# Turning a tile's gathered rows with a DMA transposition instead of TensorE, in a GRU scan that feeds a mixture of experts

## What is computed

```python
# x: [16, 256, 512]; h starts from cond_2048 [16, 512]; D = 512
def cell(h, x):                        # GRU, 256 steps, one after the other
    gi = x @ W_ih + b_ih               # [16, 1536]
    gh = h @ W_hh + b_hh
    r, z = sigmoid(i_r + h_r), sigmoid(i_z + h_z)
    n = tanh(i_n + r * h_n)
    return (1.0 - z) * n + z * h
# the 4096 rows h go through a mixture of 8 experts, top 2 of 8, hidden width 352
scores = h @ Wg.T;  w = softmax of the two best scores
for e in range(8):
    y += w[:, e] * ((silu(h @ W1[e].T) * (h @ W2[e].T)) @ W3[e].T)
out = x + y
```

## Time and profile before

| | us |
|---|---|
| median of 3 runs | 1501.19 (1500.92 to 1502.19) |
| span of the profiled execution | 1501.1 |
| TensorE matmuls, busy | 1409.4 (94% of the span) |
| VectorE, busy | 1043.8 (70%) |
| ScalarE, busy | 896.3 (60%) |
| GpSimd, busy | 415.8 (28%) |

### The profile page before, as it was taken

The page is one execution under the profiler, slowest core; times in us unless marked ns, Lnnn a source line. Parts: engine busy times, 40 slices in busy tenths (PEclk is TensorE's granted clock), DMA queues, the critical chain, the costliest instruction groups (busy, mean ns, idle before and its releaser), DMA issues.

```text
span 1501.1 us, 88729 instructions
## 1 busy us (share of the span) xinstructions
PE 1409.4 (94%) x37804; PEld 1227.2 (82%) x37804; DVE 1043.8 (70%) x4116; ACT 896.3 (60%) x2319; POOL 415.8 (28%) x850
## 2 busy tenths in 40 slices
PE   2888878899999999999999999999999999998997
PEld 1888778888888888888888888888888888885664
DVE  7788887777677677777777767776777776764333
ACT  6677675555565556655556555665556655555664
POOL 1011112123322232222332223222333222326443
PEclk9999887899999999999999999999999999999999
DMA  8445413112221222212222122211222212223431
GB/s 290 124 130 140 134 45 90 40 32 40 46 39 39 46 46 40 39 39 46 40 46 40 39 46 46 41 38 40 46 40 46 40 39 47 39 40 79 60 49 16
DMA packets 99011, 88.64 MB, mean 59 GB/s; under 512 B 41407, under 2 KB 74175, under 8 KB 98624
## 3 DMA queue, kind: packets, MB, share of 16 engines
q0 software_dynamic: 17952, 33.64, 12.9%
q1 hardware_dynamic: 80672, 49.32, 11.5%
HBM read 59.12 MB, written 35.72 MB: 63 GB/s over the span
## 4 chain that ended last, share of the span: by engine, by line
PE 83%; DVE 10%; issue 3%; ACT 1%; POOL 1%; DMA 1%; SPq 0%; DVEq 0%; POOLq 0%; ACTq 0%
PE gn_bank L1366 12%; PE gz_ps L1366 12%; PE y_ps L1458 9%; PE b_ps L1388 9%; PE a_ps L1422 8%; PE b_ps L1422 8%; PE gi_ps L1388 8%; PE gr_ps L1357 6%; PE gr_ps L1351 6%; DVE wexp L1037 2%; PE tr_ps L1436 2%; PE tr_ps L1446 2%; PE tr_ps L1478 1%; DVE npre L1067 1%; DVE nmh L1073 1%
## 5 line engine op out<-in xcount | busy, mean ns | idle before, releaser
L1366 PE MATMUL gz_ps<-hlog,whh 128*128 128x32 f16 x8192 | 246.0, 177 | 6.1 <-issue 6.0
L1366 PE MATMUL gn_bank<-hlog,whh 128*128 128x32 f16 x8192 | 245.2, 177 | 2.4 <-issue 2.2
L625 POOL DMA_INDIRECT out_y<-work,mt x57 | 93.9, 1648 | 546.2 <-PE gz_ps L1366 309.6
L1366 PEld LDWEIGHTS gz_ps<-hlog,whh 128*128 128x128 f16 x8192 | 224.1, 96 | 6.9 <-issue 6.7
L1366 PEld LDWEIGHTS gn_bank<-hlog,whh 128*128 128x128 f16 x8192 | 224.2, 96 | 2.7 <-issue 2.7
L1351 PEld LDWEIGHTS gr_ps<-hlog,whh 128*128 128x128 f16 x4096 | 130.6, 96 | 53.9 <-DVE hlog L1080 32.4
L1351 PE MATMUL gr_ps<-hlog,whh 128*128 128x16 f16 x4096 | 141.9, 170 | 31.3 <-DVE hlog L1080 28.3
L1388 PE MATMUL b_ps<-xs,wih 128*128 128x64 f16 x4752 | 162.3, 197 | 3.4 <-issue 2.1
L1458 PE MATMUL y_ps<-wexp,work 128*128 x639 | 159.0, 382 | 1.9 <-ACT work L845 1.9
L1388 PEld LDWEIGHTS b_ps<-xs,wih 128*128 128x128 f16 x4752 | 153.3, 101 | 5.1 <-issue 3.5
L810 ACT ACTIVATE rs<-rpre,sc 128x64 f32<-128x64 f32 x256 | 88.0, 344 | 112.7 <-DVE rpre L1054 112.5
(11 more groups left out here) (217 smaller groups left out, 2550.3 us busy)
## 6 DMA issues: line engine op xcount, KB each, us to landing
wexp<-in_w_units SPq DMA_DIRECT2D x46, 256.0 KB, 3.8
x_raw<-in_x_feat SPq DMA_DIRECT2D x32, 256.0 KB, 3.7
out_y<-in_x_tok SPq DMA_DIRECT2D x16, 512.0 KB
h_tok<-xrow SPq DMA_DIRECT2D x32, 256.0 KB, 2.0
wexp<-in_w_hh SPq DMA_DIRECT2D x4, 768.0 KB, 6.8
wexp<-in_w_inproj SPq DMA_DIRECT2D x4, 768.0 KB, 11.8
wexp<-in_w_units SPq DMA_DIRECT2D x15, 192.0 KB, 4.5
mt<-meta SPq DMA_DIRECT2D x71, 1.0 KB, 1.7
```

The lines of the kernel that those rows point to most:

```text
L625: pool.indirect_dma_start(out=out, out_offset=bass.IndirectOffsetOnAxis(ap=mt[:, j % RING, 0:1].bitcast(I32), axis=0), in_=ysc[y_slot(j)], ...
L1366: mm = pe.matmul(dst[:, j], whh[:, i, k, m * P:(m + 1) * P], h[:, k], start=False, stop=True, skip_group_check=True)
```

## The change

The block X disappears from TensorE and `take_x` from ScalarE. SyncE issues one DMA transposition a tile, `turn_gathered(j)`, from xg to xT, two steps before the tile's block A. It waits until the gather has landed and until block B of the tile that used the same xT buffer has ended. Block A and the gather into the same xg buffer now wait for its semaphore. In the tail SyncE's loop is: turn_gathered(j), then take_up(j+2). The inner activations (T) and the rows of h (R1) are turned on TensorE as before.

```diff
         if g >= 0 and s in (2, ranked):
             work += [("R1" if s == 2 else "R2", g)]
-        if (t + 1 - FIRST) % CYCLE == 0 and t + 1 >= FIRST:
-            work += [("X", (t + 1 - FIRST) // CYCLE)]
...
         if j + 1 < TILES:
-            tail += [("E", j + 1), ("X", j + 1)]
+            tail += [("E", j + 1)]
...
-        x_mm = sem("x_mm")
-        x_taken = sem("x_taken")
+        gathered_turned = [sem(f"gathered_turned_{i}") for i in range(2)]
...
+            def turn_gathered(j):
+
+                sp.wait_ge(x_gathered[j % 4], 16 * (j // 4 + 1))
+                if j:
+                    sp.wait_ge(b_mm, j if j <= MAIN_TILES else j - 1)
+                sp.dma_start_transpose(xT[x_slot(j)], xg[g_slot(j)]).then_inc(gathered_turned[j % 2], 16)
+
...
                         take_up(j)
                         if j == MAIN_TILES:
                             take_up(j + 1)
-
-            for j in range(MAIN_TILES + 2, TILES):
-                if stage(j) == LAST and stage(j - 1) < LAST:
-                    store_rows(LAST)
-                take_up(j)
+                    elif t == base(j) - 2:
+                        turn_gathered(j)
+
+            take_up(MAIN_TILES + 2)
+            for j in range(MAIN_TILES + 1, TILES):
+                turn_gathered(j)
+                if j + 2 < TILES:
+                    if stage(j + 2) == LAST and stage(j + 1) < LAST:
+                        store_rows(LAST)
+                    take_up(j + 2)
...
                 if j - 3 > MAIN_TILES:
-                    pool.wait_ge(x_mm, j - 3 - MAIN_TILES)
+                    pool.wait_ge(gathered_turned[(j - 3) % 2], 16 * ((j - 3) // 2 + 1))
                 elif j > MAIN_TILES:
                     pool.wait_ge(gi_mm, GI_BATCHES)
                 elif j:
-                    pool.wait_ge(tr_mm, TR_NO["X", j - 1] + 1)
+                    pool.wait_ge(gathered_turned[(j - 1) % 2], 16 * ((j - 1) // 2 + 1))
...
-            def take_x(j):
-                if j:
-                    act.wait_ge(b_mm, j if j <= MAIN_TILES else j - 1)
-                dst = xT[x_slot(j)].rearrange("p c t -> p (c t)")
-                if j <= MAIN_TILES:
-                    act.wait_ge(tr_mm, TR_NO["X", j] + 1)
-                    S.copy(dst, tr_ps[:]).then_inc(tr_taken, 1)
-                else:
-                    act.wait_ge(x_mm, j - MAIN_TILES)
-                    S.copy(dst, gn_bank[:].bitcast(F16)).then_inc(x_taken, 1)
...
                 if w == 0:
-                    if j <= MAIN_TILES:
-                        pe.wait_ge(tr_taken, TR_NO["X", j] + 1)
-                    else:
-                        pe.wait_ge(x_taken, j - MAIN_TILES)
+                    pe.wait_ge(gathered_turned[j % 2], 16 * (j // 2 + 1))
...
-            def turn_x(j):
-                pe.wait_ge(x_gathered[j % 4], 16 * (j // 4 + 1))
...
-                for c in range(2 * K):
-                    mm = pe.transpose(dst[:, c * P:(c + 1) * P], xg[g_slot(j)][:, c * P:(c + 1) * P], ident[:])
-                mm.then_inc(tr_mm if j <= MAIN_TILES else x_mm, 1)
```

More of the change, by code:

```diff
@@ L156, in gru_moe_kernel @@
             tail += [("T", j - 1)]
-    TR_NO = {b: n for n, b in enumerate([b for b in main + tail if b[0] in ("T", "R1")
-                                              or b[0] == "X" and b[1] <= MAIN_TILES])}
+    TR_NO = {b: n for n, b in enumerate([b for b in main + tail if b[0] in ("T", "R1")])}
     ROUTED_BEFORE_A, BATCH_BEFORE_B, B_BEFORE_BATCH = {}, {}, {}
@@ L925, in _ @@
                     probabilities(t // GS - 1)
-                if t >= FIRST - 1 and s == CYCLE - 1:
-                    take_x(j + 1)
                 if t % GS == 6 and t // GS + 2 < UNITS_X:
@@ L938, in _ @@
                 gate_sigmoid(j)
-                if j + 1 < TILES:
-                    take_x(j + 1)
                 if j > MAIN_TILES:
@@ L1531, in run @@
                     turn_hidden(n)
-                elif kind == "X":
-                    turn_x(n)
                 elif kind == "D0":
```

## The result

The changed kernel takes 1490.42 us (median of 5, 1489.49 to 1497.22) beside 1501.19 of the kernel before (1499.14 to 1502.82, timed again on the same chip). The ratio is 0.9943 [0.992, 0.9965]: 8.6 us by the ratio and 10.8 by the medians, where 25.5 were forecast. The time lies in the slower part of the stated range and the sign was right, but the gain is only a third to two fifths of what the sum promised.

A forecast was written before the change was run, and what follows sets the result against it. TensorE's queue was taken to bound scan and steady tail. Scan -21.4 and tail -4.1 (head +2.5, steady tail -6.6) sum to -25.5 us from 1501.1: 1475.5 us forecast, range 1470 to 1497 (80%).

The forecast's parts named there:

- Block X, 0.42 us x 51 = 21.4: Scan: each removed block of TensorE transpositions frees 0.42 us, for 51 blocks 21.4 us; bounds 18.4 to 23.5.
- L = 5.0: DMA transposition's time from issue on SyncE to its semaphore, taken as 5.0 us, between estimates 3.4 and 5.7.
- the 1024 pieces: Assumption that a transposition reads 1024 pieces of 256 B, 128 rows by eight blocks of 128 columns.
- Hidden in the scan: Scan: transposition starts some 12 us before block A wants it, so L up to 12 us costs nothing.
- The added DMA traffic ... nothing: Scan: 1024 more packets in 20 us beside a DMA share of 0.21 were costed at nothing.
- The steady tail, 6.6: Behind A(55): 15 tile periods, each 0.44 us shorter without X, gain 6.6 us.
- The head, +2.5: Start of the tail: A(55) starts 2.5 us later because transpositions delay the chain of gathers.
- 2L - 7.5: Tail's head: delay of A(55), transposition paid twice, in GpSimd's queue and between gather and A.
- gives nothing: Last scan step: removing the 52nd block, X(51), gains nothing, since R1 behind it waits for H_LO anyway.
- The drain behind the last tile is the same: End of the kernel: the time behind the last tile was taken as unchanged.
- about 10 us of the 11.7 that two tiles last: Steady tail: mt and gather behind the transposition take about 10 us of 11.7, so hidden without much room.
- SyncE held so long in issuing that mt is late: Listed sign that the forecast is wrong: SyncE's issuing of transpositions makes the row-number load mt late; no size given.

The follow-up runs named there:

- e2: Kernel before with DMA transposition only for tail tiles 52 to 70, TensorE still turning the scan's tiles: ratio 1.0041 to the kernel before.
- e14: Kernel before with the scan's 51 DMA transpositions added and TensorE's block X kept: ratio 1.0019 to the kernel before.
- e9: Changed kernel run again unedited, on another set's chip: ratio 0.9936 to the kernel before.
- e1: Changed kernel with the tail of before: DMA transposition only for scan tiles 0 to 51: ratio 0.9922 to the kernel before.
- e15: Scan-only kernel again (DMA transposition in the scan, TensorE turning the tail), in another set: ratio 0.9909 to the kernel before.
- e3: Changed kernel with mt issued ahead of the transposition in the tail, last h_tok store and transposition 54 before the list wait: ratio 0.9879 to the kernel before.
- e6: Changed kernel with GpSimd's tail loop issuing add_rows(j-2) ahead of gather(j+4): ratio 0.9884 to the kernel before.
- e12: Scan-only kernel with no turning of rows in the scan at all, so output differs: ratio 1.0406 to the kernel before.
- e7: Changed kernel with gather(53) waiting until transposition 52 has ended: ratio 0.9904 to the kernel before.
- e8: Changed kernel with both tail reorderings, mt ahead of the transposition and add ahead of the gather: ratio 0.9886 to the kernel before.
- e10: Changed kernel with gather(53) waiting for transposition 52 and tail adds issued ahead of gathers: ratio 0.9871 to the kernel before.
- e11: Scan-only kernel with each scan transposition replaced by a plain copy of the same 256 KB, rows unturned: ratio 0.9907 to the kernel before.

## Why the forecast missed

- **Block X, 0.42 us x 51 = 21.4:** right. It took 21.2 (before) and 20.9 (e2) of TensorE, and the step behind it moves up by all of that.
- **L = 5.0:** right, 4.7 in the scan and 4.4 over all, and so were the 1024 pieces behind it. Hidden in the scan: right, no wait of block A for it shows there.
- **"The added DMA traffic ... nothing":** wrong. The forecast asked who waits for the transfer, and not whom it delays. By e14 some 3 us, by the other pairs up to 5, of the 21.4 come back in stops of TensorE. That TensorE waits in such stops for its instruction packets is seen in the traces, before and after; that the transpositions lengthen the packets rests on 1.90 us against 1.67 at the same place, and is argued from there. The rest of the 6.2 us that the scan gives back is stops as well, but the runs can't say whose.
- **The steady tail, 6.6:** near. T to T is 5.85; the whole stretch from A(55) to the last T shrinks by 5.1 in the first profile and 6.2 in e9.
- **The head, +2.5:** too small; +4.2 in the mean, +6.3 in the first profile. "2L - 7.5" has the right chain, but L was taken as the same everywhere, and this one transposition ran beside a gather (10.0). TensorE's longer stops there also bring the clock to 0.5, which was not in the sum. And that the 52nd block, X(51), "gives nothing" seems too kind: in the kernels without it the clock falls there, and in e1 and e15 A(55) comes 2.6 us later.
- **"The drain behind the last tile is the same":** wrong, and shown by e3 and e6: +5.4. The forecast saw mt come late ("about 10 us of the 11.7 that two tiles last") and followed it to the gather, but not to what stands behind the gather on GpSimd. The add isn't on TensorE's path, so nothing shows until TensorE has ended, and then the backlog is paid in full. "SyncE held so long in issuing that mt is late" stood among the forecast's own signs of being wrong, and it is near to what came: mt is late, but by the transposition's landing and not by its issue.

The sum of the tail is thus +4.2 - 5.6 + 5.4 = +4.0 where -4.1 stood, and the scan's -14.8 where -21.4 stood: -10.8 in all. The drain (5.4) and the scan's give-back (6.2) are of one size; no single step explains the miss. That -10.8 is also the difference of the medians is in part luck: by the ratios it is 8.6 us in the first set of runs and 9.7 in the second.

The Trainium skill (DMA: Bandwidth & Descriptors, Latency and other measured facts) gives an effective 261 GB/s for DMA transpositions with a non-contiguous middle dimension. The trace does not reach that: 256 KB in 4.7 us, with mt's 1.7 taken off, are an estimated 87 GB/s for one transposition at a time. No run here keeps several of them in flight.

Still open: what e12's stops are, and the last step, which is 2 to 3.5 us longer in e3, e6, e7, e8, e9, e10 and e11, where VectorE's reduction for z or n starts 1.5 to 3.2 us late and no record shows for what (e9's waits, the stretch of its last step):

```profile
DVE zpre L1047 <- remote: 3.2, 1, 3.2
```

## What to carry to other kernels

Work moved from the bounding engine to a DMA queue gives what it took on that engine; then ask whom the transfer delays, instruction loads included, and not only who waits for it. When something on a queue comes later, follow every instruction behind the one that waits, also those off the critical path: a backlog there is paid at the end, as 5.4 us here, and a change of order in a few lines took nearly all of it away. Before a slow packet is put down to the new transfer, look at the same place in the kernel without it. And one profile of a scan like this can be off by some 4 us either way.

## What the runs showed of the hardware

- A transposition of 256 KB of 16-bit values from SBUF to SBUF, 1024 packets of 256 B and 32 of 4 B, lands in 3.0 us at the least, 4.4 in the median (after); 10.0 beside a gather (8.8 in e2), at most 5.1 when that gather waits (e7). Its issue keeps SyncE for 1.27 us.
- TensorE's instructions come in packets of 16 KB that take 1.1 us. Outside e12, 353 of the 430 stops of over 0.2 us without a semaphore end 1.2 to 1.7 us behind the end of such a packet. Where a gather has just landed the packets take 1.67 us (before and e2), and 1.90 when a transposition starts there as well.
- One program gave 0.9887 and 0.9879 of before on two chips and 1.0406 on a third, by stops of 0.54 us inside blocks and the fall of the clock behind them.
- TensorE's eight transpositions of 128x128 keep it for 0.42 us in a full queue.
